# Nine field pairs copied by DMA, four spread by TensorE: a recommendation network on one core

## The reference

```python
emb = tables[feat_idx, sparse]                       # 2048 x 26 x 32
linear_out = lin_sparse_w[feat_idx, sparse].sum(-1) + dense @ lin_dense_w
x0 = emb; xk = emb
for w, bb in ((conv1_w, conv1_b), (conv2_w, conv2_b)):
    h = xk.shape[1]
    hp = einsum('bhd,bmd->bhmd', xk, x0).reshape(-1, h * M, E)
    xn = sigmoid(einsum('oi,bid->bod', w, hp) + bb[None, :, None])
    xk, res = xn[:, :64], res + [xn[:, 64:]]
cin_out = concat(res, 1).sum(-1) @ cin_w + cin_b
deep_x = concat([emb.reshape(-1, 26 * 32), dense], -1)
h3 = tanh(tanh(tanh(deep_x @ W1 + b1) @ W2 + b2) @ W3 + b3)
out = linear_out + cin_out + (h3 @ deep_w + deep_b) + bias
```

## Time and profile before

| | |
|---|---|
| median of 3 runs | 1645.41 us (1644.03 to 1645.74) |
| the profiled execution | 1642.12 us |
| its span, first to last instruction | 1640.3 us |
| granted TensorE clock | 0.995 of full |
| PE busy | 1566.3 us (95%) |
| DVE, ACT, POOL busy | 1143.2, 704.7, 763.8 us |

### The profile page before, as it was taken

The page is one execution under the profiler, slowest core; times in us unless marked ns, Lnnn a source line. Parts: engine busy times, 40 slices in busy tenths (PEclk is TensorE's granted clock), DMA queues, the critical chain, the costliest instruction groups (busy, mean ns, idle before and its releaser), DMA issues.

```text
span 1640.3 us, 23407 instructions
## 1 busy us (share of the span) xinstructions
PE 1566.3 (95%) x6840; PEld 681.2 (42%) x6840; DVE 1143.2 (70%) x992; ACT 704.7 (43%) x981; POOL 763.8 (47%) x631
## 2 busy tenths in 40 slices
PE   0599999999999999999999999999999997999998
PEld 0233333333333333333333333333333336787876
DVE  3287878787878787878787878787878783434432
ACT  1344444343444444444344444343444424444543
POOL 7657474757474656565655655664742010000000
PEclk9999999999999999999999999999999999999999
DMA  4688787888887888888888888888888762232231
GB/s 93 124 195 199 189 198 192 194 193 191 196 194 194 194 194 190 193 188 193 195 194 194 194 191 192 193 195 193 196 194 193 185 150 92 92 101 86 89 107 39
DMA packets 111803, 277.60 MB, mean 169 GB/s; under 512 B 26036, under 2 KB 46804, under 8 KB 111704
## 3 DMA queue, kind: packets, MB, share of 16 engines
q1 hardware_dynamic: 98456, 270.11, 66.0%
q0 software_dynamic: 13312, 7.06, 5.3%
HBM read 270.03 MB, written 7.04 MB: 169 GB/s over the span
## 4 chain that ended last, share of the span: by engine, by line
PE 94%; POOL 2%; DVE 1%; ACT 1%; issue 1%; DMA 0%; ACTq 0%; DVEq 0%; POOLq 0%
PE y L636 45%; PE xn L630 21%; PE bc L750 16%; PE bc L616 5%; PE bc L623 3%; PE bc L599 2%; POOL emb L443 2%; PE bc L608 1%; DVE xb L554 0%; ACT sq L806 0%; DVE hp L554 0%; DVE x_lo L563 0%; PE xn L767 0%; DMA sum<-sparse 0%; DMA emb<-table,idx_stage 0%
## 5 line engine op out<-in xcount | busy, mean ns | idle before, releaser
L554 DVE TENSOR_TENSOR hp<-bc,xk 128x1024 f32<-128x1024 f32 x384 | 448.9, 1219 | 264.2 <-PE bc L616 264.2
L554 DVE TENSOR_TENSOR xb<-xb,xk 128x1024 f32<-128x1024 f32 x448 | 581.4, 1355 | 22.8 <-ACT xk L811 22.8
L443 POOL DMA_INDIRECT emb<-table,idx_stage x416 | 495.8, 1192 | 145.9 <-issue 130.5
L636 PE MATMUL y<-xb,w2s 128*64 128x512 f32 x1792 | 423.6, 599 | 0.3 <-ACT r L816 0.3
L636 PE MATMUL y<-hp,w2s 128*64 128x512 f32 x1536 | 368.2, 600 | 0.0
L630 PE MATMUL xn<-sq,w1s 128*128 128x512 f32 x768 | 363.0, 609 | 5.4 <-ACT sq L806 3.2
L806 ACT ACTIVATE sq<-bc 128x1024 f32<-128x1024 f32 x192 | 182.9, 1027 | 261.3 <-PE bc L623 261.3
L810 ACT ACTIVATE xk<-xn,bias 64x512 f32<-64x512 f32 x128 | 87.3, 682 | 376.4 <-PE xn L630 376.4
L458 POOL TENSOR_TENSOR r<-r 128x512 f32<-128x512 f32 x96 | 148.7, 1549 | 144.1 <-ACT r L816 98.4
L630 PEld LDWEIGHTS xn<-sq,w1s 128*128 128x128 f32 x768 | 136.6, 191 | 183.3 <-issue 157.1
L636 PEld LDWEIGHTS y<-xb,w2s 128*64 128x64 f32 x1792 | 117.2, 136 | 214.6 <-issue 188.3
(11 more groups left out here) (63 smaller groups left out, 1056.4 us busy)
## 6 DMA issues: line engine op xcount, KB each, us to landing
xb<-x_rows SPq DMA_DIRECT2D x896, 256.0 KB, 4.9
w_raw<-W SPq DMA_DIRECT2D x32, 448.0 KB, 3.3
w_raw<-W SPq DMA_DIRECT2D x16, 512.0 KB, 3.3
emb<-table,idx_stage POOLq DMA_INDIRECT x416
x_rows<-deep_t SPq DMA_DIRECT2D x16, 384.0 KB
w_raw<-W SPq DMA_DIRECT2D x8, 256.0 KB, 2.7
hp<-select SPq DMA_DIRECT2D x2, 512.0 KB, 4.8
x_rows<-deep_t SPq DMA_DIRECT2D x16, 45.0 KB
```

Of the source, the lines that this page charges most:

```text
L443: nc.gpsimd.indirect_dma_start(out=emb[:, m, :], out_offset=None, in_=table, in_offset=bass.IndirectOffsetOnAxis(ap=idx_stage[:, m:m + 1], ...
L554: nc.vector.tensor_tensor(product(n)[:, :], x[:, :], xk[sl % 2][:, :], ALU.mult).then_inc(multiplied, 1)
L636: last = nc.tensor.matmul(y2[H * c:H * c + H, :], w2s[:, ORDER[n], :], src[:, c * CHUNK:(c + 1) * CHUNK], start=(n == 0), stop=(n == PAIRS ...
```

## The change

- Pairs: `BY_PE` shrinks from six to four pairs (two quads a step, not three), `BY_DMA` grows from seven to nine. The order of pairs and `STEP_WORK` are rewritten: both quads are placed otherwise, five contractions of the last step stand at the start of a step.
- A pair's two fields now sit in quarters of the 128 partitions: the second field in partitions 32 to 95, the first in 0 to 31 and 96 to 127 (`PAIR_ROWS`). So a pair is copied by three DMAs (64, 32 and 32 partitions) instead of two of 64.
- `make_high`, `make_low`, `turn_x0` and the copy of `x0t` go. In their place ACT writes, beside `deep_t`, an upper half of the turned embeddings (`turned_deep`), DVE the lower half (`lower_deep`), SP dumps both to HBM (`dump_halves`, four DMAs a tile) and loads the rows of a step back as `x0t` (`load_rows`, four DMAs a step, 26 partitions each).
- The turn of the dense embeddings moves from step 2 of a tile to step 1, and stands directly ahead of the first quad.
- The deep network's `x_hi` and `x_lo` are loaded by DMA from the dumped halves (`load_x`, 16 DMAs a group) instead of being made by ACT and DVE; the first group's load and weights are placed ahead of the last steps. The dense inputs are split and dumped in the prologue.
- At the end, the linear terms and the first sum are added within the last step, and one ACT instruction reads the result instead of four.

```diff
-ORDER = [3, 10, 4, 0, 7, 11, 5, 1, 8, 2, 9, 12, 6]
-BY_PE = (3, 4, 7, 8, 9, 10)
+ORDER = [0, 1, 2, 8, 3, 4, 5, 9, 6, 10, 7, 11, 12]
+BY_PE = (2, 3, 10, 11)
...
 STEP_WORK = (
     ("fill", (("K", 0), ("K", 1), ("K", 2))),
-    ("of_last", (9, 10, 11, 12)),
-    ("fill", (("T", 0), ("D", 0), ("D", 1))),
+    ("of_last", (8, 9, 10, 11, 12)),
+    ("fill", (("D", 0), ("D", 1))),
+    ("fill", (2, 3)),
     ("first", 0),
-    ("fill", (3, 4)),
-    ("of_this", (0, 1, 2)),
+    ("of_this", (0, 1, 2, 3, 4)),
     ("first", 1),
-    ("fill", (7, 8)),
-    ("of_this", (3, 4)),
-    ("fill", (9, 10)),
-    ("of_this", (5, 6, 7, 8)),
+    ("fill", (10, 11)),
+    ("of_this", (5, 6, 7)),
 )
...
-SL_DEEP = 2
+SL_DEEP = 1
...
+PAIR_ROWS = ((1, slice(QUARTER, 3 * QUARTER)), (0, slice(0, QUARTER)), (0, slice(3 * QUARTER, P)))
...
+            def load_rows(t, sl):
+                for half in range(2):
+                    rows = x0_halves[bass.ds(t, 1), half, :, :].rearrange("t (m e) b -> (t m) e b", e=ROW)
+                    for c in range(2):
+                        first = sl * STEP_D + c * Q
+                        start = H * c + half
+                        sp.dma_start(x0t[sl][start:start + 2 * M:2, :].bitcast(F32),
+                                     rows[:, first:first + Q, :].rearrange("m d b -> m (d b)")).then_inc(x0_loaded[sl % 2], 16)
...
             def spread_by_dma(t, sl, i):
-                for f in range(2):
+                for f, parts in PAIR_ROWS:
                     first = (2 * ORDER[BY_DMA[i]] + f) * ROW + sl * STEP_D
                     row = x0_rows[bass.ds(t, 1), first:first + STEP_D, :].rearrange("t d b -> t (d b)")
-                    sp.dma_start(xb[i][H * f:H * f + H, :], row.to_broadcast([H, COLS])).then_inc(spread[i], 16)
+                    sp.dma_start(xb[i][parts, :], row.to_broadcast([parts.stop - parts.start, COLS])).then_inc(spread[i], 16)
...
                         spread_by_dma(t, sl, i)
+
+
+                        if i == 2 and sl == SL_DEEP + 1 and ahead > 0:
+                            dump_halves(t + 1)
+                        if i == 3 and sl == SL_DEEP + 1 and ahead > 0:
+                            await_halves(t + 1)
+                        if i == 3 and (sl < 2 or ahead > 0):
+                            if is_first and sl == 0:
+                                sp.wait_ge(filled, PRO_FILLS)
+                            load_rows(t + (sl + 2) // STEPS, (sl + 2) % STEPS)
+                    if sl == SL_DEEP and ahead > 0:
+                        dump(t + 1)
+                    if sl == 2 and ahead == 0:
+                        sp.wait_ge(dense_dumped, 64)
+                        load_x(0, 0, 1)
...
-                elif is_t(held):
-                    pe.wait_ge(x0t_copied, s + 3)
                 else:
-                    pe.wait_ge(deep_copied, t * 2 + (3 + held[1]))
+                    pe.wait_ge(deep_rounded, t * DEEP_N + (DEEP_N + held[1] + 1))
```

More of the change, by code:

```diff
@@ L122 @@
 TILE_FILLS = sum(len(step_fills(sl, 1)) for sl in range(STEPS))
-assert TILE_FILLS % SLOTS == 0 and PRO_FILLS % SLOTS == 0
-AHEAD = 6, 14, 20
+assert TILE_FILLS % SLOTS == 0
+AHEAD = 8, 16, 23
 assert AHEAD[-1] <= M
+ROW_LOADS = 4
 def feature_pairs():
@@ L159, in build @@
         idf = sb("idf", [P, P])
-        w_raw = [sb("w_raw0", [P, F1N // P, P])]
+        w_raw = [sb(f"w_raw{i}", [P, F1N // P, P]) for i in range(2)]
         bd1 = sb("bd1", [P, F1N // P])
@@ L299, in build @@
         GATHERED = 16 * M
+        DEEP_N = len(DEEP_PARTS)
         FOLDS = 2
         SUMS = STEPS - 1 + FOLDS
[L304 to L308, removed]
         def over_tiles(eng, tile):
@@ L393, in tile @@
                     s = t * STEPS + sl
-                    if sl == SL_DEEP + 1 and ahead > 0:
-                        dump(t + 1)
                     for i, n in enumerate(BY_DMA):
@@ L594, in _ @@
         def _(pe):
-            def turn_x0(slot, sl):
-                for q in range(Q):
-                    d = sl * STEP_D + 2 * q
-                    last = nc.tensor.matmul(bc[slot][:, q * P:(q + 1) * P],
-                                            halves[:, d:d + 2, :, :, :].rearrange("p c g i m -> p (c g i m)"),
-                                            idr[:, :], start=True, stop=True)
-                last.then_inc(filled, 1)
             def turn_deep(slot, ks):
-                rows = emb[:, 0:M, :].rearrange("p m e -> p (m e)")
+                rows = emb[:, :, :].rearrange("p m e -> p (m e)")
                 for at, k in enumerate(ks):
@@ new lines, in _, with turned_deep @@
+            upper_w(0, 0)
+            def turned_deep(slot, t, part, is_first=False):
+                ks = DEEP_PARTS[part]
+                whole = len(ks) if ks[-1] < KD - 1 else len(ks) - 1
+                pieces = [(slice(0, P), ks[0], ks[0] + whole, 0)]
+                if whole < len(ks):
+                    pieces.append((slice(0, LAST_E), KD - 1, KD, whole * P))
+                if part == 0 and not is_first:
+                    act.wait_ge(dumped, t * (16 * DUMPS))
+                    act.wait_ge(halves_dumped, t * (32 * DUMPS))
+                for rows, k, k_end, at in pieces:
+                    src = bc[slot][rows, at:at + (k_end - k) * P].rearrange("p (k b) -> p k b", b=P)
+                    last = nc.scalar.activation(deep_t[rows, k:k_end, :], src, ACT.Copy)
+                last.then_inc(deep_copied, 1)
+                for rows, k, k_end, at in pieces:
+                    src = bc[slot][rows, at:at + (k_end - k) * P].rearrange("p (k b) -> p k b", b=P)
+                    last = nc.scalar.activation(deep_halves[rows, 0, k:k_end, :], src, ACT.Copy)
+                last.then_inc(deep_rounded, 1)
```

357 lines of the change are left out of this document (185 added, 172 removed).

## The result

The changed kernel takes 1904.13 us (median of 4 runs, 1898.83 to 1908.58), the kernel before 1645.58 us (1644.03 to 1645.77): 1.157 times as long, 95% interval 1.154 to 1.160. Forecast were 1733 us and a range up to 1815. The profiled execution has a span of 1897.0 us, 256.7 more than before.

The account below looks back on a forecast made before the run. PE bound the kernel before; SP's DMA issues were to bind the loop after. 13 tiles at +7.75 us give +101, with the smaller terms +88, from the median 1645.4 to 1733 us; range 1660 to 1815.

Parts of the forecast that it names:

- A tile of the loop: Loop over 13 tiles: SP's issues, dumps and wait need 88.3 us a tile, 7.75 above the 80.55 before.
- the third issue: Last of a pair's three copies on SP, without address arithmetic ahead: taken as 0.50 us, between 0.455 and 0.72.
- Loads of rows: SP's four loads a step from the dumped halves: 0.72 us each, 2.9 us a step (0.5 to 0.72 each).
- Wait for the halves: SP stands still behind the dump of the halves until it lands: 2.6 us a tile, bounds 0.9 and 6.
- SP's slack on entering the loop: Buffers free some 10 us early, copies land in 4.9: 5 us are eaten before anyone waits, -5 us.
- The high end: SP's need per tile in the loop with every free term at its high end: 99 us.
- SP's case: SP's issues bind the loop: chance 0.62, own range 1690 to 1775 us.
- The written-out tiles: Three tiles outside the loop: SP under 19 us a step, so 11 full steps save 0.93 us each, -10.
- DMA at the mixed price: Rival: middle copy at 3.14 us per MB, others at 4.12; DMA engines bind at 83.5 us a tile, 1693 us; chance 0.13.
- Prologue: Before the squares' matmuls: turn, splitting, dumps and loads take about 15 us instead of 8.2, +7 us.
- Into the deep network and tail: After the last contraction: first accumulation runs at once, -8 us; at the end two terms and one ACT read, -4.5.
- The rival in which PE stays the bound: SP and the DMA engines both stay below PE's 78.0 us a tile: faster, 1604 us; chance 0.13.

Follow-up runs that it names:

- at half width: The changed kernel with SP's program written out, and every copy of a row narrowed to the first half of its columns: 1654.70 us, 81.2 us a tile.
- the kernel with seven pairs: The changed kernel, but seven pairs by DMA in two copies and six by PE in three quads: 1626.73 us, 0.989 of the kernel before.

## Why the prediction was wrong

The mechanism was right: SP's issues became the bound, SP stopped waiting for contractions, PE idles 13.8 us per 100, nearly all of it behind a DVE that waits for copies, and the time is above before. The size was too small by 169 us of 257. Its steps, with tiles in the loop taken between back-edges and the others from first convolution to first convolution:

- **A tile of the loop**, forecast 88.3 us, measured 98.4 (99.0 in the tile shown). In it: 36 pairs 70.3 (forecast 69.8), right, the third issue 0.54 us with the little between. Loads of rows 16.9 (11.5): mis-sized. I took the 0.72 of a copy for them, as if an issue cost the same whatever its shape, and had 0.72 for the upper end; it is 1.02 to 1.1, and their stepped partitions are the reason (0.75 us an issue against 0.37 for adjacent ones, alone). Dumps 4.9 (4.3). Wait for the halves 2.0 (2.6). And 4.8, on average 4.3, at the back-edge, for which there was no term: the kernel before has no such gap (0.23 us), because its loop is short enough: 236 recorded instructions, and padded to 420 it has one of 2.4 us. That is 10.1 us a tile, 131 us in 13. The first of them took only 91.9 us, which is SP's slack on entering the loop: 13 tiles took 228 us more than before, where 101 less 5 of slack were forecast.
- **The bounds of this step were the second fault.** The high end was put at 99 us, and the mean came out at 98.4, but the range on record reached only to 1815, which is 94.6 a tile. It followed the own range of SP's case instead of its ends. That 98.4 lies below 99 is luck besides: the 99 came from a dear third issue and a long wait for the halves, and neither occurred, while the two terms that did grow were outside their bounds or had none. Even 99 us a tile would have made the sum 1872.
- **The written-out tiles**, forecast 0.93 us a step faster than before. They were slower: tile 0 took 86.7 us (76.7 before, from first convolution to first convolution), tile 14 86.5 (80.6), and tile 15 to the last contraction 107.3 (92.3). The prediction had the DMA engines at 83.5 us a tile, above PE's 78.0, and yet priced these tiles at PE's. This is an error in the working, not in a row: where SP doesn't bind, the next bound is the DMA engines, not PE. About 33 us: 12 in tile 0, 8 in tile 14, 13 in tile 15. The full engines are seen in tiles 14 and 15 only. In tile 0 their share is 0.83 (65 to 151 us), and with the row loads by ACT the tile takes 78.3 us at 0.90 (65 to 143 us), while with SP written out it takes 86.4 us, and 76.3 at half width: SP's queue and the bytes both have a part in it, and how they divide stays open. Of tile 15's part some is not theirs either, since the kernel with seven pairs, whose share is 0.91 there, takes 101.4.
- **DMA at the mixed price**, 83.5: nearly right. Tiles at full engines take 86.5 to 88 us, the pair's three copies alone went at 251 GB/s where the two prices together make 275, and in the loop the share of 0.84 of 98.4 us is 83. The price alone was never what the loop waited for.
- **Prologue** +7.4 (forecast +7). **Into the deep network and tail**: from the last contraction to the end of the span 276.7 us against 286.5, -9.8 (forecast -12.5). The first deep matmul follows the last contraction without a gap.

Together 131 + 33 + 3 = 167 of the 169. The experiments on the cause agree: half of the bytes bring next to nothing, taking 16 loads away from SP 11.3 us a tile, taking arithmetic and back-edge away 10.1 us a tile, and these two stop where the DMA engines are full, at 87 to 88. How the 10.1 us divide between arithmetic and gap in this kernel was not measured apart; the added terms give 4.3 for the gap, and the rest is hidden by the DMA engines becoming the bound.

The rival in which PE stays the bound is out: 130 issues fill a tile of 98 us, and PE is busy 344.64 of 400 us.

## What to carry to other kernels

An engine that only issues DMAs can set the pace like the others (here 130 issues filled a tile of 98.4 us): count its issues a round, by shape, with the register arithmetic between them, and put that beside the slowest engine before splitting one copy into more. Where the DMAs of a loop outgrow one sequencer, give some to an engine that is idle, or write the issuing engine's loop out; both cost a few lines here and gave 141 to 169 us. Neither brought nine copied pairs below the kernel before, because the DMA engines were full next (shares of 0.98 and 0.99); of the whole kernels here only the one with seven pairs is faster than it. And after each bound that is taken away, price the rest at the next one, not at the engine that one hopes for.

## What the runs showed of the hardware that was not expected

- In these kernels a loop body of SP with 313 recorded instructions or more pays 2.4 to 8.1 us on average at a back-edge and brings five fetches a round; one with 298 or fewer pays 0.24.
- An issue of 26 rows to every second partition takes 0.75 us, to adjacent partitions 0.37, for the same 52 KB; 32 rows to every second partition take 0.59.
- On one chip more than 100 of SP's register instructions take 0.1 to 0.98 us, not 0.03 to 0.08, in each of the three kernels profiled there; the kernel before takes 1666.1 us on it and 1644.6 to 1645.6 elsewhere.
- Copies to 64 partitions go at 209 GB/s into 0 to 63 and at 353 into 32 to 95. Mixed with two copies to 32 partitions each, the pair goes at 251; two halves in turn go at 234.
